# Reordering scatters, pad writes and pair statistics in a one-core conv, attention and expert kernel

## The chip, the cores and the metric

The kernel runs on one core of one Trainium2 chip. The metric is the device time of one execution in microseconds (us). The time before is the median of three runs. Engines are named as in the profile: PE is the matrix engine, DVE the vector engine, ACT the scalar engine, POOL the GpSimd engine and SP the sync engine, which here only issues DMAs.

## The reference

The input x is 32 x 64 x 16 x 16. Three blocks follow each other, all in float32:

```python
x = x + _L0_conv_ref(_gn(x), ...)      # group norm of channel pairs, depthwise 3x3 conv (all weights come out as 1)
t = _to_tokens(x)                      # 8192 tokens of 64 channels
t = t + _L1_attn_ref(_ln_t(t), ...)    # hash buckets, pooled keys and values, 8 heads, GELU feed-forward of 256
t = t + _L1_ffn_ref(_ln_t(t), ...)     # router over 8 experts, top 2, SiLU-gated experts of 682 hidden units
x = _from_tokens(t, x)
```

In the attention block each token picks one of 8 buckets in each of 4 hashes (an argmax over rotated features). The means of the buckets give 32 keys and values per image, and a query attends over them. In the expert block each token goes to its two best experts, each result times its gate.

## The kernel before, in words

The 32 images are taken in 8 groups of 1024 tokens. Every group passes four stages: **a** (group norm, convolution, first layer norm), **b** (buckets, keys, values, scores, attention), **c** (second half of the attention, feed-forward) and **d** (router, places of the rows). The program is a software pipeline written out by hand: in round i group i is in stage a, group i-1 in b, group i-2 in c and group i-3 in d. Each engine has its own list of steps per round and runs it strictly in that order, and semaphores tie the lists together. A step that waits holds up everything behind it on its engine.

Rounds 0 to 4 (`iteration`, run by `ramp`) have no expert work: these are the rounds without tiles. Rounds 5 to 9 (`mixed_iteration`, run by `mix`; MIX is 5) also compute experts. The routed rows (the token twice, the gate and the token's number: 130 floats) are scattered to DRAM by POOL with indirect DMAs (`scatter`, L538), 16 of them for each group. Experts then work on tiles of 256 rows: 71 tiles, cut into two bursts per round. For a tile SP loads weights (`load_weights`, L412) and rows (`load_rows`, L423) three tiles ahead; PE turns the rows (`turn_rows`, L831), ACT copies them (`store_xs`), PE does the up products (`up`, L876), ACT the SiLU (L1135), DVE the product (L1558), PE the down product (L889). POOL scatters the results (L546). The first row load waits until all 16 scatters of group 1 have landed; these are spread over rounds 4 and 5.

Behind each expert's last row the kernel writes a pad of 256 rows, so that its last tile reads harmless rows, and one more pad behind all regions: nine DMAs on SP (`write_pad`, L382). Their places are known once DVE has counted the last group (`pads_ready`, L1522). The first tile that can touch a pad is tile 49, and its row load waits for all nine.

The steps of the pair statistics belong to stage a. `pair_means` and `pair_variances` are two tiny products on PE (L644, L648); `channel_variances` (L1306 to L1308) lies between them on DVE and `pair_statistics` (L1312, L1313) behind them; POOL's `group_rstd` (L482 to L487, a power) follows, then ACT's `normalise_x` (L1027). In stage b, `rotate` (L681) leads to `buckets` (L1355 to L1360), `bucket_sums` (L697), `bucket_means` (L1366 to L1369), `turn_pooled` (L703), `store_pooled` (L1374), `keys` and `values` (L708, L714); `queries` (L688) are copied by ACT (`store_queries`, L1055). In stage c, `sum2`, `total2` and `centre2` (L1405 to L1413) on DVE are followed by `squares2` on ACT (L1087), `variance2` on DVE (L1419, L1420), and the power `rstd2` on POOL (L499). ACT's list has `squares2` and, from round 3 on, `store_wtok` (L1107, which the router's product waits for) ahead of `store_queries`.

Of the kernel before, what the change touches and what calls it, by code (L numbers as in the profile page):

```python
# [19 lines left out]
NE = 8  # L20
# [52 lines left out]
def hybrid_block(nc, x, consts, smalls, weights, out):  # L73
    with ExitStack() as ctx:
# [310 lines left out]
        def _(sp):  # L385
# [14 lines left out]
            def write_pads():  # L400
                sp.wait_ge(pads_ready, 1)
                write_pad(sp, NE * REG)
                for e in range(NE):
                    write_pad(sp, sp.value_load(pad_row[0:1, e:e + 1], min_val=0, max_val=NE * REG - MT))
# [28 lines left out]
            def burst(i, part):  # L433
                for t in range(*BURSTS[i, part]):
                    if t == PADS_AT:
                        write_pads()
                    load_tile(t + W_SLOTS - 1)
# [19 lines left out]
        def _(pool):  # L457
# [118 lines left out]
            def mixed_iteration(i, a=None, b=None, c=None, d=None):  # L576
                if i == MIX:
                    run(c, residual)
                    scatter(MIX - 4, 5, 3)
                    run(d, rstd3)  # L580
                    scatter(MIX - 4, 8, 2)
                    run(c, rstd2)
                    run(a, group_rstd)
                    scatter(MIX - 4, 10, 6)
                    run(b, unit_sum)
                else:
                    run(a, group_rstd)
                    if i == MIX + 1:
                        scatter(MIX - 2, 8, 4)
# [40 lines left out]
        def _(pe):  # L630
# [282 lines left out]
            def iteration(i, a=None, b=None, c=None, d=None, e=None):  # L913
                run(c, attend, 2)
                run(c, attend, 3)
                run(b, turn_n1, 1)
                run(a, pair_means)
                run(b, rotate)
                run(a, pair_variances)
                run(d, turn_wtok)  # L920
                run(b, queries, 0)
                run(b, queries, 1)
# [25 lines left out]
            def mixed_iteration(i, a=None, b=None, c=None, d=None):  # L948
                if i == MIX:
# [16 lines left out]
                    turn_rows(BURSTS[i, 0][0])  # L966
                    turn_rows(BURSTS[i, 0][0] + 1)
                    run(c, fc1, 1)
                    run(c, fc2, 0)
                    run(c, fc2, 1)  # L970
                else:
# [48 lines left out]
        def _(act):  # L1020
# [159 lines left out]
            def mixed_iteration(i, a=None, b=None, c=None, d=None):  # L1180
                if i == MIX:
# [10 lines left out]
                    run(b, key_blocks)  # L1192
                    store_xs(BURSTS[i, 0][0])
                    store_xs(BURSTS[i, 0][0] + 1)
                    run(c, gelus, 1)
# [67 lines left out]
        def _(dve):  # L1263
# [321 lines left out]
            def iteration(i, a=None, b=None, c=None, d=None, e=None):  # L1585
# [7 lines left out]
                run(c, attended, 1)  # L1593
                run(c, sum2)
                run(c, total2)
                run(c, centre2)
                run(d, normalise3)
                run(a, channel_variances)
                run(b, buckets)
                run(a, pair_statistics)  # L1600
                run(c, variance2)
                run(b, bucket_means)
# [124 lines left out]
def run(group, step, *args):  # L1727

    if group is not None:
        step(group, *args)  # L1730
# [37 lines left out]
PADS_AT = BURSTS[NG + 1, 1][0] + 4  # L1768
# [89 lines left out]
```

## Time and profile before

| | |
|---|---|
| median of 3 runs | 767.5 us (766.65 to 769.26) |
| the profiled execution | 771.0 us, its span 769.1 us |
| PE | busy 633.8 us (82%), mean granted clock 0.897 |
| DVE | busy 479.8 us (62%) |
| POOL | busy 369.3 us (48%) |
| ACT | busy 364.0 us (47%) |
| pads | nine DMAs of 130 KB |

The span runs from the first to the last instruction. A granted clock of 1.00 is 2.4 GHz, of 0.50 it is 1.2 GHz. In a row of the timeline the first number is the start, the second the duration, both in us, and the brackets give the idle time before it and what ended that. PE's matmuls are counted as passes there (an fp32 product has two), and neighbouring rows of one kind are merged. The rounds without tiles lie at about 34 to 71 (round 1), 71 to 104 (round 2), 104 to 144 (round 3) and 144 to 187 us (round 4); round 5 up to its first tile lies at 187 to 229 us; the last burst (tiles 40 to 70) begins at 582 us.

### The profile page before, as it was taken

What the parts mean: (1) busy time and instruction counts of PE and PEld (TensorE: products, weight loads), DVE (VectorE), ACT (ScalarE), POOL (GpSimd) and SP (SyncE); (2) the same over time, 40 slices, a digit from 0 to 9 for tenths busy, and PEclk for the clock granted to TensorE, in tenths of its full rate; (3) what the DMA queues carried; (4) which work ended last, traced back from release to release, by engine and by line L of the source; (5) the groups of instructions that cost most, each with busy time, mean ns of one, the idle gap of its engine ahead of it and who ended that gap; (6) DMA issues with size and microseconds to landing.
All of it is one profiled execution on the core that took longest, in us unless ns stands there. A gap on an engine that the chain in (4) does not pass through costs nothing.

```text
span 769.1 us, 14151 instructions
## 1 busy us (share of the span) xinstructions
PE 633.8 (82%) x4582; PEld 474.5 (62%) x4582; DVE 479.8 (62%) x1206; ACT 364.0 (47%) x710; POOL 369.3 (48%) x378
## 2 busy tenths in 40 slices
PE   2497889798559798889999999978978989999950
PEld 1476768667346675658657776756566657777730
DVE  2337677778408775578767877586756535555535
ACT  1133636465426364555557555654554435555520
POOL 2202250776702727764874558444755724444450
PEclk9658887879559899999999999999997989999985
DMA  2000000011132313352341416051542655555509
GB/s 85 5 15 1 15 0 15 18 46 60 35 121 83 124 37 111 117 146 90 107 149 54 160 60 187 18 158 37 183 130 63 188 159 165 161 164 161 165 6 327
DMA packets 46617, 75.50 MB, mean 98 GB/s; under 512 B 7488, under 2 KB 30048, under 8 KB 46544
## 3 DMA queue, kind: packets, MB, share of 16 engines
q1 hardware_dynamic: 35600, 57.67, 25.2%
q0 software_dynamic: 8640, 12.74, 4.8%
q10 hardware_dynamic: 2304, 4.20, 1.4%
q8 instruction: 37, 0.61, 0.3%
q14 instruction: 36, 0.29, 0.1%
HBM read 58.56 MB, written 16.47 MB: 98 GB/s over the span
## 4 chain that ended last, share of the span: by engine, by line
PE 42%; issue 17%; POOL 16%; DVE 15%; ACT 4%; DMA 4%; SPq 2%; POOLq 0%; ACTq 0%; DVEq 0%
PE bk L876 15%; POOL expert_rows L538 9%; PE bk L889 9%; DVE units L1558 3%; PE bk L786 3%; PE bk L660 2%; PE bk L831 2%; PE bk L751 2%; PE bk L725 2%; POOL rr L493 2%; POOL expert_results L546 2%; PE bk L896 1%; PE bk L776 1%; POOL r L499 1%; PE bk L681 1%
## 5 line engine op out<-in xcount | busy, mean ns | idle before, releaser
L876 PE MATMUL bk<-xs,wbuf 64*128 64x256 f32 x1704 | 209.9, 390 | 9.7 <-DVE units L1558 6.1
L546 POOL DMA_INDIRECT expert_results<-yout,xin x142 | 140.8, 992 | 144.8 <-DVE yout L1569 112.7
L1558 DVE TENSOR_TENSOR units<-bk,silu 128x512 f32<-128x512 f32 x213 | 143.9, 689 | 89.1 <-ACT silu L1135 88.5
L876 PEld LDWEIGHTS bk<-xs,wbuf 64*128 64x128 f32 x1704 | 161.6, 189 | 55.0 <-issue 27.0
L1135 ACT ACTIVATE silu<-bk 128x512 f32<-128x512 f32 x213 | 125.1, 596 | 84.9 <-PE bk L876 84.5
L538 POOL DMA_INDIRECT expert_rows<-srow,pos x128 | 130.7, 1021 | 70.7 <-issue 36.0
L889 PE MATMUL bk<-units,wbuf 128*64 128x256 f32 x852 | 108.9, 391 | 3.9 <-DVE ysum L1565 3.5
L889 PEld LDWEIGHTS bk<-units,wbuf 128*64 128x64 f32 x852 | 55.5, 137 | 39.8 <-issue 11.8
L1129 ACT ACTIVATE ysb<-bk 128x256 f32<-128x256 f32 x71 | 27.3, 384 | 86.0 <-PE bk L889 86.0
L493 POOL TENSOR_TENSOR rr<-vare,c_mhalf 128x16 f32<-128x16 f32 x8 | 23.5, 2937 | 83.1 <-DVE vare L1338 83.1
L831 PE MATMUL bk<-const,xin 128*128 128x128 f32 x142 | 30.0, 304 | 22.2 <-DMA xin<-expert_rows 15.1
L831 PEld LDWEIGHTS bk<-const,xin 128*128 128x128 f32 x142 | 15.7, 147 | 44.1 <-issue 26.4
L751 PE MATMUL bk<-vblk,prob_t 128*128 128x144 f32 x256 | 38.1, 302 | 2.9 <-ACT prob_t L1082 2.9
L725 PE MATMUL bk<-kblk,qt 65*128 65x256 f32 x128 | 35.4, 406 | 6.1 <-DVE ssub L1390 6.0
L751 PEld LDWEIGHTS bk<-vblk,prob_t 128*128 128x128 f32 x256 | 34.5, 199 | 6.5 <-ACT prob_t L1082 6.4
L1124 ACT ACTIVATE xs<-bk 128x256 f32<-128x256 f32 x71 | 26.2, 381 | 22.7 <-PE bk L831 22.7
L786 PEld LDWEIGHTS bk<-small,hid 128*128 128x128 f32 x256 | 32.1, 204 | 4.8 <-ACT hid L1098 4.5
L786 PE MATMUL bk<-small,hid 128*128 128x128 f32 (+1 forms) x256 | 32.9, 288 | 2.1 <-ACT hid L1098 2.1
L1075 ACT ACTIVATE prob<-ssub 128x512 f32<-128x512 f32 x32 | 19.7, 627 | 31.0 <-DVE ssub L1390 30.9
L660 PE MATMUL bk<-const,hsum 128*128 128x128 f32 x192 | 34.2, 327 | 0.0
L1563 DVE COPY ysum<-bk 128x128 f32<-128x128 f32 x71 | 20.1, 283 | 22.2 <-PE bk L896 21.6
L504 POOL TENSOR_TENSOR r<-vare,c_mhalf 128x8 f32<-128x8 f32 x8 | 13.8, 1724 | 39.3 <-DVE vare L1439 39.2
(192 smaller groups left out, 979.8 us busy)
## 6 DMA issues: line engine op xcount, KB each, us to landing
wbuf<-in_weights SPq DMA_DIRECT2D x71, 576.0 KB, 4.0
xin<-expert_rows SPq DMA_DIRECT2D x71, 130.0 KB, 3.4
expert_results<-yout,xin POOLq DMA_INDIRECT x142, 3.1
xg<-in_x SPq DMA_DIRECT2D x8, 256.0 KB, 2.8
expert_rows<-srow,pos POOLq DMA_INDIRECT x128, 2.4
srow<-expert_results SPq DMA_DIRECT2D x8, 256.0 KB, 5.3
srow<-expert_results ACTq DMA_DIRECT2D x8, 256.0 KB, 6.3
out<-hid ACTq DMA_DIRECT2D x8, 256.0 KB, 5.6
```

Source lines behind the costliest of these rows:

```text
L493: g.tensor_tensor(rr[:, :, :].rearrange("p a j -> p (a j)"), vare1[:, :, :].rearrange("p a j -> p (a j)"), c_mhalf[:, :], ALU.pow).then_in ...
L538: g.indirect_dma_start(rows[0:NE * REG, :], bass.IndirectOffsetOnAxis(ap=pos[:, d, k, j:j + 1], axis=0), srow[:, d % ROW_SLOTS, k, j, :], ...
L546: g.indirect_dma_start(results[:, :], bass.IndirectOffsetOnAxis(ap=xin[:, t % X_SLOTS, h, ROW - 1:ROW].bitcast(U32), axis=0), yout[:, t % ...
L660: last = mm(o, hsum[:, s, h0 + dy:h0 + dy + 8, :], ident, start=False, stop=dy == 2)
L725: last = mm(bk12[:, p % 2, bp * 256:(bp + 1) * 256], qt[:, j * P:(j + 1) * P], kblk[:, m, :, :].rearrange("c h m -> c (h m)"), start=True, ...
L751: last = mm(bk5[:, at:at + 2 * (C + HEADS)].rearrange("p (r c) -> p r c", r=2), prob_t[:, p % 2, 2 * bp + ch, :], vblk[:, m, ch, :].unsque ...
L786: last = mm(y_of(c)[:, j:j + n, :], hid[:, a, par, q * P:(q + 1) * P], fc2_s[:, a, :].unsqueeze(1).broadcast_to([P, n, C]), start=a == 0, ...
L831: last = turn(xt_of(t)[:, h * P:(h + 1) * P], xin[:, t % X_SLOTS, h, 0:2 * C], ident)
L876: last = mm(bank[:, ch * MT:(ch + 1) * MT], wbuf[part, t % W_SLOTS, at:at + P], xs[part, t % 2, :], start=True, stop=True)
L889: last = mm(y_bank(t)[ch * C:(ch + 1) * C, 0:MT], wbuf[:, t % W_SLOTS, at:at + C], units[:, t % 2, q, ch * MT:(ch + 1) * MT], start=q == 0 ...
L1135: f(silu[:, q, :], h1_ps[q], ACT.Silu).then_inc(silu_ready, 1)
L1558: tt(units[:, t % 2, q, :], h3_ps[q], silu[:, q, :], ALU.mult).then_inc(unit_ready, 1)
```

## The change: what it does

There are four parts.

1. **Pads.** The nine pad writes stood together ahead of the loads of tile 47. Now two stand ahead of the loads of each of tiles 44, 45, 46 and 47, and the ninth ahead of those of tile 48.
2. **Scatters of round 5.** The last eight scatters of group 1 stood as two, then the two powers `rstd2` and `group_rstd`, then six. Now all eight stand ahead of the powers.
3. **First rows of round 5.** `turn_rows` of tiles 0 and 1 moves on PE from between the two halves of `fc1` to behind `fc2`; on ACT `store_xs` moves behind the second `gelus`.
4. **Rounds without tiles.** On PE `rotate` now stands ahead of `pair_means` and `queries` ahead of `pair_variances`. On DVE `buckets`, `channel_variances` and `normalise3` now stand ahead of `sum2`, `total2` and `centre2`, and `bucket_means` ahead of `variance2`.

```diff
-            def write_pads():
+            def write_pads(k):
                 sp.wait_ge(pads_ready, 1)
-                write_pad(sp, NE * REG)
-                for e in range(NE):
+                if k == PAD_STEPS:
+                    write_pad(sp, NE * REG)
+                for e in range(2 * k, min(2 * k + 2, NE)):
                     write_pad(sp, sp.value_load(pad_row[0:1, e:e + 1], min_val=0, max_val=NE * REG - MT))
...
-                    if t == PADS_AT:
-                        write_pads()
+                    if PADS_AT <= t <= PADS_AT + PAD_STEPS:
+                        write_pads(t - PADS_AT)
                     load_tile(t + W_SLOTS - 1)
...
                     run(d, rstd3)
-                    scatter(MIX - 4, 8, 2)
+                    scatter(MIX - 4, 8, 8)
                     run(c, rstd2)
                     run(a, group_rstd)
-                    scatter(MIX - 4, 10, 6)
                     run(b, unit_sum)
...
                 run(b, turn_n1, 1)
+                run(b, rotate)
                 run(a, pair_means)
-                run(b, rotate)
+                run(b, queries, 0)
+                run(b, queries, 1)
                 run(a, pair_variances)
                 run(d, turn_wtok)
-                run(b, queries, 0)
-                run(b, queries, 1)
                 run(b, bucket_sums)
...
                     run(c, fc1, 0)
-                    turn_rows(BURSTS[i, 0][0])
-                    turn_rows(BURSTS[i, 0][0] + 1)
                     run(c, fc1, 1)
                     run(c, fc2, 0)
                     run(c, fc2, 1)
+                    turn_rows(BURSTS[i, 0][0])
+                    turn_rows(BURSTS[i, 0][0] + 1)
...
+                    run(c, gelus, 1)
                     store_xs(BURSTS[i, 0][0])
                     store_xs(BURSTS[i, 0][0] + 1)
-                    run(c, gelus, 1)
...
                 run(c, attended, 1)
+                run(b, buckets)
+                run(a, channel_variances)
+                run(d, normalise3)
                 run(c, sum2)
                 run(c, total2)
                 run(c, centre2)
-                run(d, normalise3)
-                run(a, channel_variances)
-                run(b, buckets)
                 run(a, pair_statistics)
+                run(b, bucket_means)
                 run(c, variance2)
-                run(b, bucket_means)
...
-PADS_AT = BURSTS[NG + 1, 1][0] + 4
+PADS_AT = BURSTS[NG + 1, 1][0] + 1
+PAD_STEPS = NE // 2
```

**POOL, round 5.** Before, between `residual` (x2t) and `unit_sum`; L504 is `rstd3`, L499 `rstd2`, L482 to L487 `group_rstd`:

```order
L538 DMA expert_rows<-srow,pos 67584x130 x3
L504 TENSOR_TENSOR r<-vare,c_mhalf 128x8
L538 DMA expert_rows<-srow,pos 67584x130 x2
L499 TENSOR_TENSOR r<-vare,c_mhalf 128x8
L482 TENSOR_TENSOR grstd<-gvar,c_mhalf 128x2
L484 TENSOR_SCALAR rstd<-grstd 128x2
L485 TENSOR_TENSOR gshift<-gneg,grstd 128x2
L487 TENSOR_SCALAR shift_b<-gshift,small 128x2
L538 DMA expert_rows<-srow,pos 67584x130 x6
```

And now (lines below L406 are counted one higher in the new file):

```order
L539 DMA expert_rows<-srow,pos 67584x130 x3
L505 TENSOR_TENSOR r<-vare,c_mhalf 128x8
L539 DMA expert_rows<-srow,pos 67584x130 x8
L500 TENSOR_TENSOR r<-vare,c_mhalf 128x8
L483 TENSOR_TENSOR grstd<-gvar,c_mhalf 128x2
L485 TENSOR_SCALAR rstd<-grstd 128x2
L486 TENSOR_TENSOR gshift<-gneg,grstd 128x2
L488 TENSOR_SCALAR shift_b<-gshift,small 128x2
L516 TENSOR_TENSOR u_tok<-u_tok,u 128x512
```

Six scatters moved from behind the two powers to ahead of them.

**PE, round 5.** The end of the list up to the first tile (L776 is `fc1`, L786 `fc2`), as a piece of the difference:

```order
 L761 MATMUL bk<-const,n 128x128 x4
 L714 MATMUL bk<-v_aug,pooled_rep 128x128 x4
-L776 MATMUL bk<-n2t,fc_s 128x512 x2
-L831 MATMUL bk<-const,xin 128x128 x4
-L776 MATMUL bk<-n2t,fc_s 128x512 x2
+L776 MATMUL bk<-n2t,fc_s 128x512 x4
 L786 MATMUL bk<-small,hid 128x128 x14
 L786 MATMUL bk<-small,hid 128x64 x2
+L831 MATMUL bk<-const,xin 128x128 x4
 L876 MATMUL bk<-xs,wbuf 128x256 x24
```

The four turns of the first two tiles' rows moved from the middle of `fc1` to just ahead of the tiles.

**DVE, round 2.** Before, from `attended` to `pair_statistics`:

```order
L1399 TENSOR_TENSOR att<-bk,rden 128x256
L1405 TENSOR_TENSOR x<-u,att 128x512
L1410 TENSOR_REDUCE ssum<-x 128x8
L1413 SCALAR_TENSOR_TENSOR cent<-ssum,x 128x512
L1306 TENSOR_TENSOR dmean<-mv,bk 128x2
L1307 TENSOR_TENSOR dmean<-dmean 128x2
L1308 TENSOR_TENSOR chvar<-dmean,mv 128x2
L1355 TENSOR_REDUCE bmax<-bk 128x32
L1356 TENSOR_TENSOR beq<-bk,bmax 128x256
L1358 TENSOR_TENSOR beq<-beq,const 128x256
L1359 TENSOR_REDUCE bfirst<-beq 128x32
L1360 TENSOR_TENSOR onehot<-beq,bfirst 128x256
```

And now (one higher again):

```order
L1356 TENSOR_REDUCE bmax<-bk 128x32
L1357 TENSOR_TENSOR beq<-bk,bmax 128x256
L1359 TENSOR_TENSOR beq<-beq,const 128x256
L1360 TENSOR_REDUCE bfirst<-beq 128x32
L1361 TENSOR_TENSOR onehot<-beq,bfirst 128x256
L1307 TENSOR_TENSOR dmean<-mv,bk 128x2
L1308 TENSOR_TENSOR dmean<-dmean 128x2
L1309 TENSOR_TENSOR chvar<-dmean,mv 128x2
L1406 TENSOR_TENSOR x<-u,att 128x512
L1411 TENSOR_REDUCE ssum<-x 128x8
L1414 SCALAR_TENSOR_TENSOR cent<-ssum,x 128x512
L1313 TENSOR_SCALAR gvar<-bk 128x2
```

The five bucket steps and the three of the channel variances moved ahead of the three that end in the centred tokens (`cent`), and these now stand ahead of `gvar`.

## Rows read from the trace of the kernel before

**Rows 1.** Timeline of SP, 590 to 620 us:

```profile
593.43 0.37 SPq L423 DMA_DIRECT2D xin<-expert_rows  x1
597.14 0.35 SPq L412 DMA_DIRECT2D wbuf<-in_weights  x1
...
603.82 9.99 SPq L382 DMA_DIRECT2D expert_rows<-const  x9
614.65 0.37 SPq L412 DMA_DIRECT2D wbuf<-in_weights  x1
615.80 0.40 SPq L423 DMA_DIRECT2D xin<-expert_rows  x1
```

**Rows 2.** Timeline of PE, 605 to 630 us (L876 starts a tile, L831 turns rows):

```profile
605.89 2.86 PE L876 MATMUL bk<-xs,wbuf 64*128 64x256 f32 x24
...
610.71 2.86 PE L876 MATMUL bk<-xs,wbuf 64*128 64x256 f32 x24
619.07 0.69 PE L831 MATMUL bk<-const,xin 128*128 128x128 f32 x2 [5.50 <-DMA xin<-expert_rows]
...
628.26 2.86 PE L876 MATMUL bk<-xs,wbuf 64*128 64x256 f32 x24
```

**Rows 3.** The row loads (L423), 590 to 640 us:

```profile
DMA to landing us min/median/max: 3.2/3.6/4.2
```

**Rows 4.** Timeline of POOL, round 5:

```profile
195.77 1.44 POOL L538 DMA_INDIRECT expert_rows<-srow,pos  x1 [0.19 <-issue]
...
199.35 1.67 POOL L499 TENSOR_TENSOR r<-vare,c_mhalf 128x8 f32<-128x8 f32 x1 [0.88 <-DVE vare L1420]
...
208.26 0.96 POOL L538 DMA_INDIRECT expert_rows<-srow,pos  x1 [0.31 <-issue]
209.52 0.96 POOL L538 DMA_INDIRECT expert_rows<-srow,pos  x1 [0.30 <-issue]
```

**Rows 5.** Timeline of PE, round 5 up to the first tile:

```profile
203.68 1.08 PE L761 MATMUL bk<-const,n 128*128 128x128 f32 x4 [0.24 <-DVE lsub L1452]
...
206.40 2.08 PE L776 MATMUL bk<-n2t,fc_s 64*128 64x512 f32 x4
...
218.56 0.69 PE L831 MATMUL bk<-const,xin 128*128 128x128 f32 x2 [3.09 <-DMA xin<-expert_rows]
219.18 2.08 PE L776 MATMUL bk<-n2t,fc_s 64*128 64x512 f32 x4
222.61 6.39 PE L786 MATMUL bk<-small,hid 128*128 128x128 f32 x32 [1.35 <-ACT hid L1098]
```

**Rows 6.** Timeline of ACT, the same stretch:

```profile
209.67 2.14 ACT L1069 ACTIVATE kblk<-bk,const 65x128 f32<-65x128 f32 x8
...
222.58 1.28 ACT L1135 ACT_TABLE_LOAD   x1
230.10 0.60 ACT L1135 ACTIVATE silu<-bk 128x512 f32<-128x512 f32 x1 [6.24 <-PE bk L876]
```

**Rows 7.** Windows: us, busy us (instructions) of PE, PEld, DVE, ACT, POOL; PE clock; DMA share; GB/s:

```profile
85.00:105.00 20.00, 19.22 (x139) 16.32 (x137) 14.92 (x31) 12.66 (x20) 3.80 (x2) 1.00 0.00 1
```

**Rows 8.** Timeline of ACT, round 2:

```profile
76.13 0.59 ACT L1055 ACTIVATE qt<-bk 65x512 f32<-65x512 f32 x1 [1.18 <-PE bk L688]
```

**Rows 9.** Timeline of DVE, rounds 2 and 4:

```profile
73.59 0.69 DVE L1413 SCALAR_TENSOR_TENSOR cent<-ssum,x 128x512 f32<-128x512 f32 x1
...
149.05 1.76 DVE L1445 TENSOR_TENSOR wtok<-cent,r 128x512 f32<-128x512 f32 x1 [1.57 <-POOL r L504]
...
159.81 0.23 DVE L1451 TENSOR_REDUCE lmax<-bk 128x8 f32<-128x64 f32 x1 [1.21 <-PE bk L804]
```

**Rows 10.** Timeline of POOL, round 4:

```profile
150.34 1.59 POOL L515 TENSOR_TENSOR u_tok<-u_tok,u 128x512 f32<-128x512 f32 x1
```

**Rows 11.** Timeline of PE, round 4 (the wait for the channel variances):

```profile
145.78 2.03 PE L681 MATMUL bk<-rot_aug,n1t 65*128 65x128 f32 x16
152.20 0.58 PE L648 MATMUL bk<-chvar,const 128*128 128x2 f32 x2 [4.39 <-DVE chvar L1308]
```

## The prediction

> **What bounds the kernel now.** I read the windows first, for the clock and for who is busy where; then the list of waits for each stage; then the timelines around the four places that the change touches. The reader is to see that each stage has its own limit.
>
> In the last burst PE is the limit: a tile takes 610.71 - 605.89 = 4.82 us from one start to the next [rows 2]. One place falls out of this beat: PE stands 5.50 us until the rows of tile 47 land [rows 2]. The reason is on SP. The nine pads occupy it from 603.82 to 613.81, 1.11 us each, and the loads of tile 47 stand behind them: weights at 614.65, rows at 615.80, landed 3.3 us later [rows 1, 2].
>
> In round 5, up to the first tile, the limit is POOL. The last scatter of group 1 starts at 209.52 [rows 4]; only then may SP load the first rows; those of tile 1 are turned at 218.56; the second `fc1` half stands behind that turn, then `gelus`, `fc2` (222.61 to 229.00), and the first tile [rows 5]. PE idles or runs at 1.2 GHz: its 32 passes of `fc2` take 6.39 us.
>
> In the rounds without tiles nothing is saturated. A chain runs through PE, DVE, POOL and ACT, and PE waits in it for the channel variances, 4.39 us in round 4 [rows 11].
>
> **The change part by part.** Times are those of the profiled execution (771.0 us, span 769.1); the median is 3.5 us less, and I carry differences over unchanged. From 230 us on the program only follows its own dependencies, so whatever is gained ahead of that shifts everything behind it.
>
> *Pads.* Tile 46 starts at 610.71 and tile 48 at 628.26. Without the stall tile 48 would start two beats behind tile 46: 610.71 + 2 x 4.82 = 620.35. The loss is 628.26 - 620.35 = 7.9 us: 5.5 of standing, the rest PE work at the lower clock behind it [rows 2]. Now two pads (2 x 1.11 = 2.2 us) go into SP's gap of each tile. The gap is there: the rows of tile 44 are issued at 593.43 (to 593.80) and the weights of tile 45 at 597.14, 3.3 us later [rows 1]. Of these about 0.84 us is the lead-in of a load, as between 613.81 and 614.65, so two pads fill 593.8 to 596.0 and the lead-in ends at 596.9: just inside. The rows have slack too: tile 45's, issued at about 598.3, take 3.2 to 4.2 us to land [rows 3] and are needed 2 us ahead of the tile start at 605.89, at 603.9, so 1.4 to 2.4 us are left. I take the whole 7.9 as gained; the bounds are -7.9 and -3 (each of four tiles slipping 1.2).
>
> The Trainium skill says in "DMA: Bandwidth & Descriptors", section "Queues, rings and completion order", that SP's DMAs share one row of rings and that descriptors on an engine are consumed in ring order, so a load behind pads also waits for their bytes, not only for SP. By the row, the rows issued behind all nine pads landed in 3.3 us, like any other [rows 1, 2], so the trace so far does not bear out a cost; by the rule two pads in front would lengthen four loads, which is the rival "late rows" below.
>
> *Scatters of round 5.* On POOL the eight scatters now run on from 195.77. The first takes 1.44, the others come every 1.26 us (209.52 - 208.26) [rows 4]: the last starts at about 205.1, 4.4 us earlier. The price: `rstd2`, done at 201.0 before, now starts at 206.1 and is done at 207.8, 6.7 us later. DVE's `normalise2` waits for it, with `centre_logits`, `value_blocks` and `centre3` queued behind. So n2 is there at 208.5, the router's bank is read out at 208.9, and `turn_n2`, at 203.68 before, starts at 209.0: +5.3 [rows 5]. `group_rstd` is also later but nobody needs it before the first burst.
>
> *First rows of round 5.* From there, with the durations of before: `values` to 212.0; `fc1` at 212.0; `key_blocks` on ACT 3.27 us behind that (209.67 - 206.40), 215.3 to 217.4; second `fc1` half at about 214.8, which no longer waits for rows; second `gelus` 217.4 to 218.7; `fc2` 218.7 to 225.1 at the low clock [rows 5, 6]. The rows landed long ago (4.4 us earlier, about 214.2), so the two turns (0.69 each) end at 226.5, and the first tile starts there, not at 229.0: -2.5. ACT's table load (1.28 us), hidden under `fc2` before, now stands behind `store_xs`: 227.0 to 228.3. The first SiLU, at 230.10 before, starts then: -1.8 [rows 6]. DVE's `centre3` follows `fc2` and is done at 227.3, earlier than that. I take -2.3 for both parts together; bounds -5 (`fc2` at 2.4 GHz) and +1 (the first tile starts at 1.2 GHz).
>
> *Rounds without tiles.* What the reader may expect is that PE's queries fill the wait for the variances, which they do. But two things come later. `pair_variances` and `pair_statistics` stand behind more work, so POOL's `group_rstd` and ACT's `normalise_x` are late. And `centre2` stands behind the buckets; ACT's `squares2` waits for it, and `store_queries` (and `store_wtok`) queue behind `squares2`.
> Round 1 has no stage c: only `normalise_x` moves, by about the duration of `queries`, 1.4 us, of which the half reaches `values`: +0.7.
> Round 2: `centre2` ended at 73.59 + 0.69 = 74.3, just as `rotate` did [rows 9]. Now, behind `rotate`, DVE does the buckets (five steps, 2.25 us), the variances (0.5) and then `sum2`, `total2` and `centre2` (2.1): it ends at 79.4. The squares end at 80.1, and the first copy of the queries starts then and not at 76.13 [rows 8]. `normalise_x`, `repeat_pooled` and `key_blocks` stand behind it, and of these 4 us about 1.6 was idle time on ACT: +2.4.
> Round 4: `rotate` (145.78 to 147.8 [rows 11], now 0.3 earlier) ends at 147.5, then the buckets at 149.8, the variances at 150.3, `normalise3` at 152.0 (at the 1.7 us that this step took at 149.05 [rows 9]), `centre2` at 154.1, the squares at 154.8, `store_wtok` at 155.3, the router's product (2.1) at 157.4. Its readout, at 159.81 before [rows 9], comes at 157.5: -2.3. Round 3 by the same steps: -1.0.
> Sum of the four: +0.7 + 2.4 - 1.0 - 2.3 = -0.2. As each is a difference of chains some 30 us long, I give it bounds of -6 and +4.
>
> How long `normalise3` takes there is open. It took 1.76 us at 149.05, while POOL was in its own adds up to 150.34 + 1.59 [rows 9, 10]; it is as large as `centre2`, 0.69 [rows 9]. By 1.7 us round 4 gives -2.3, by 0.69 it gives -3.3. The Trainium skill, "SBUF — State Buffer", section "Who interferes with whom", says that a VectorE instruction with two SBUF inputs and a GpSimd instruction that reads SBUF exclude each other for the whole instruction. The trace agrees, and by that rule it is -2.3 here too, since the step now starts right behind POOL's add at 150.34.
>
> *Sum.* -7.9 - 2.3 - 0.2 = -10.4: 760.6 for the profiled execution, 757.1 us for the median.
>
> **The rivals.**
> *Clock kept (faster).* PE's long wait in rounds 3 and 4 is broken up by queries, so the clock may not fall there. In round 4 it was at 1.2 GHz from the wait of 4.39 us on [rows 11]; `fc2`'s 32 passes show what the level costs, 6.39 us there. Some 3 us for each of the two rounds: 757.1 - 6 = 751. Against it: PE still waits, now for `squares2` and `store_wtok`, 2 us in each.
> *Late rows.* The pads lengthen the landing of four loads past their 1.4 to 2.4 us of slack, the stall comes back in pieces of 1.2 us: -3 for -7.9, 762. For it: SP's gap is full to 0.2 us; against it: the 3.3 us behind nine pads.
> *ACT's queue dominates.* The +2.4 of round 2 also holds in rounds 3 and 4, where I have -3.3 in sum: 8 us more, hence 765.
> *Slower: the clock stays down in round 2.* PE now waits at 76.5, at 78.1 and at 80.6 us for variances and queries. In 85 to 105 us PE was busy 19.22 of 20 us at a granted clock of 1.00 [rows 7]. If the clock does not come back until the round is over, this work takes about 1.75 times as long: +14, and 757.1 + 14 = 771. It decides if the level is still 0.50 behind round 2's convolution; below 10 us of such work it is no longer slower. Against it: before, the level came back behind the unbroken `values` and convolution, which are still there.
> *The change does not do what it says*: SP has no gap for two pads and one pair delays the next loads. That is "late rows" again.
>
> **How the numbers follow.** Forecast (757, own range 753.5 to 761): 0.55. Clock kept (751): 0.16. Late rows (762): 0.12. ACT's queue (765): 0.10. Slower (771): 0.07. No change is within 0.3%, 2.3 us, which is about what a measurement of this kernel can tell: 765.2 to 769.8. Half of the queue case falls there or just above its edge, and a little of the slow case: same 0.06, slower 0.06, faster 0.88. The range of 8 in 10 leaves out the slow case and the outer parts of both sides: 750 to 764.
>
> **What would show it.** In the last burst no wait of PE for rows around tile 47 and an unbroken beat of 4.8 us; SP's pads in pairs. In round 5 the last scatter 4 us before, `rstd2` 6 to 7 us later, against the round's start; PE's `fc2` no longer behind a turn, and the SiLU 2 us earlier. In round 2 ACT's `qt` some 4 us later, in round 4 the router's readout 2 us earlier. The prediction is wrong if PE still waits for rows by more than 2 us in the last burst, if the clock of rounds 2 to 4 differs by more than 5 us of low level, or if `normalise2` in round 5 is not what `turn_n2` waits for.

## The result and the profile after

| | before | after |
|---|---|---|
| median (range), 4 runs each | 768.33 us (766.65 to 769.26) | 757.06 us (753.68 to 757.51) |
| profiled execution, its span | 771.0, 769.1 us | 757.51, 755.4 us |
| PE busy, mean granted clock | 633.8 us, 0.897 | 626.2 us, 0.908 |

The ratio is 0.9845, with a 95% interval of 0.9821 to 0.9869: 11.9 us less, 10.1 to 13.8. Forecast were 757.1 us and 10.4 us less.

The table splits the two profiled executions at PE's marks: the start of the second `turn_n1` of each round, the first tile, the first tile of the last burst, and tile 48.

| stretch, us | before | after | difference |
|---|---|---|---|
| round 1 | 36.42 | 35.56 | -0.9 |
| round 2 | 32.55 | 35.46 | +2.9 |
| round 3 | 40.57 | 38.50 | -2.1 |
| round 4 | 42.82 | 41.85 | -1.0 |
| round 5 up to the first tile | 41.91 | 37.31 | -4.6 |
| first tile to last burst | 353.09 | 351.89 | -1.2 |
| last burst up to tile 48 | 46.24 | 39.47 | -6.8 |
| from tile 48 on | 140.84 | 140.82 | 0.0 |

No part of the change touches the stretch from the first tile to the last burst. In the other kernels below it is 351.95 to 354.73 us long, so its -1.2 is not put down to the change.

**The last burst.** SP's timeline of the kernel after; compare [rows 1]:

```profile
585.06 0.37 SPq L413 DMA_DIRECT2D wbuf<-in_weights  x1
586.31 0.39 SPq L424 DMA_DIRECT2D xin<-expert_rows  x1
587.77 1.56 SPq L382 DMA_DIRECT2D expert_rows<-const  x2
590.17 0.37 SPq L413 DMA_DIRECT2D wbuf<-in_weights  x1
```

The pads stand in pairs. PE's timeline, against [rows 2]:

```profile
593.77 2.86 PE L876 MATMUL bk<-xs,wbuf 64*128 64x256 f32 x24
...
596.98 0.44 PE L831 MATMUL bk<-const,xin 128*128 128x128 f32 x2 [0.35 <-DMA xin<-expert_rows]
599.01 2.86 PE L876 MATMUL bk<-xs,wbuf 64*128 64x256 f32 x24
602.90 0.44 PE L831 MATMUL bk<-const,xin 128*128 128x128 f32 x2 [1.03 <-DMA xin<-expert_rows]
604.93 2.86 PE L876 MATMUL bk<-xs,wbuf 64*128 64x256 f32 x24
```

The wait of 5.50 us is gone. Two short ones are new, 0.35 and 1.03 us, and two tiles are 5.24 and 5.92 us behind the one ahead instead of 4.82. They are waits for rows. The row loads between 570 and 640 us, against [rows 3]:

```profile
DMA to landing us min/median/max: 3.4/3.6/5.6
```

The rows of tile 45 are the 5.6: they leave at 591.38 and are turned at 596.98. Those of tile 46 are not in this list; by the chain of the trace they took 6.35 us, from 596.51 to 602.86. The loads are slower in a stretch in which the DMA engines are nearly full. Its window after (us, busy us of PE, PEld, DVE, ACT, POOL, PE clock, DMA share, GB/s):

```profile
593.00:605.00 12.00, 10.62 (x90) 7.22 (x86) 6.75 (x16) 5.12 (x10) 8.71 (x9) 1.00 0.92 255
```

and before, while the last of the nine pads went out, and then while the rows of tile 47 were on their way:

```profile
609.00:615.00 6.00, 4.57 (x40) 3.10 (x37) 3.79 (x8) 2.83 (x6) 3.80 (x4) 1.00 0.48 144
...
617.00:619.00 2.00, 0.00 (x0) 0.00 (x0) 0.00 (x0) 0.00 (x0) 0.00 (x0) 0.56 1.05 327
```

Before, the pads took the place of the loads; now they share the DMA engines with them and with POOL's scatters, at 0.92 of their time. A high share is not the whole cause, though. Before, the rows of tile 47 landed in 3.2 us while the share reached 1.05, but POOL sent nothing from 614 to 622 us. Which of the transfers holds a load up was not tried.

**Round 5.** POOL's timeline, against [rows 4]:

```profile
203.97 0.96 POOL L539 DMA_INDIRECT expert_rows<-srow,pos  x1 [0.30 <-issue]
204.95 1.67 POOL L500 TENSOR_TENSOR r<-vare,c_mhalf 128x8 f32<-128x8 f32 x1
```

The round starts at 185.91 here and at 187.02 before. Counted from there the last scatter is 4.4 us earlier and `rstd2` 6.7 us later. PE's timeline, against [rows 5]:

```profile
207.89 1.09 PE L761 MATMUL bk<-const,n 128*128 128x128 f32 x4 [5.58 <-DVE lsub L1452]
...
213.46 2.65 PE L776 MATMUL bk<-n2t,fc_s 64*128 64x512 f32 x4 [0.77 <-ACT hid L1098]
217.22 5.30 PE L786 MATMUL bk<-small,hid 128*128 128x128 f32 x32 [1.10 <-ACT hid L1098]
222.36 0.61 PE L831 MATMUL bk<-const,xin 128*128 128x128 f32 x4
223.22 5.86 PE L876 MATMUL bk<-xs,wbuf 64*128 64x256 f32 x48 [0.25 <-ACT xs L1124]
```

`turn_n2` waits 5.58 us and starts 5.3 us later than before; `fc2` starts 4.3 us earlier, no longer behind a turn; the first tile starts 4.6 us earlier. ACT's timeline, against [rows 6]:

```profile
223.46 1.28 ACT L1135 ACT_TABLE_LOAD   x1
224.75 1.09 ACT L1135 ACTIVATE silu<-bk 128x512 f32<-128x512 f32 x2
```

The table load is now in the open, and yet the first SiLU is 4.2 us earlier, counted from the round's start.

**Round 2.** ACT's timeline, against [rows 8], with DVE's step that it waits for:

```profile
78.35 0.63 ACT L1087 ACTIVATE sq<-cent 128x512 f32<-128x512 f32 x1 [6.95 <-DVE cent L1413]
78.89 1.06 ACT L1055 ACTIVATE qt<-bk 65x512 f32<-65x512 f32 x2
80.12 1.09 ACT L1027 ACTIVATE xpad<-xg,gshift,grstd 128x256 f32<-128x256 f32 x2 [0.18 <-POOL shift_b L488]
```

```profile
77.62 0.69 DVE L1413 SCALAR_TENSOR_TENSOR cent<-ssum,x 128x512 f32<-128x512 f32 x1
```

`squares2` waits 6.95 us for `centre2`, and both copies of the queries wait behind it, as expected. (In the traces DVE's lines have the same numbers as before; the second list for DVE above shows them one higher.)

**Round 4.** PE's timeline, against [rows 11]:

```profile
151.37 0.38 PE L648 MATMUL bk<-chvar,const 128*128 128x2 f32 x2 [2.03 <-DVE chvar L1308]
...
155.20 2.08 PE L804 MATMUL bk<-small,wtok_t 128*128 128x128 f32 x8 [1.57 <-ACT wtok_t L1107]
...
158.98 2.08 PE L714 MATMUL bk<-v_aug,pooled_rep 65*128 65x128 f32 x8 [0.25 <-ACT pooled_rep L1060]
```

And DVE's, against [rows 9]:

```profile
148.40 1.06 DVE L1358 TENSOR_TENSOR beq<-beq,const 128x256 f32<-128x256 f32 x1
...
149.94 0.91 DVE L1360 TENSOR_TENSOR onehot<-beq,bfirst 128x256 f32<-128x256 f32 x1
...
151.26 0.69 DVE L1445 TENSOR_TENSOR wtok<-cent,r 128x512 f32<-128x512 f32 x1
...
157.31 0.23 DVE L1451 TENSOR_REDUCE lmax<-bk 128x8 f32<-128x64 f32 x1 [1.73 <-PE bk L804]
```

The router's readout comes 2.5 us earlier than before (157.31 against 159.81; the round itself starts 0.14 us earlier), and so does `values`. Only 1.0 is left at the end of the round. From the start of `values` to `fc1` PE takes 10.77 us (158.98 to 169.75), where it took 9.30 (161.49 to 170.79): 1.5 of the 2.5 are lost there. The windows show how. After:

```profile
160.00:170.00 10.00, 10.00 (x57) 9.61 (x58) 6.88 (x25) 5.10 (x13) 7.56 (x9) 0.71 0.26 81
```

and the same stretch before:

```profile
160.00:170.00 10.00, 8.95 (x54) 8.40 (x55) 8.39 (x31) 6.99 (x19) 7.86 (x8) 0.83 0.24 75
```

And the row of `values` before, in PE's timeline:

```profile
161.49 1.16 PE L714 MATMUL bk<-v_aug,pooled_rep 65*128 65x128 f32 x8 [0.51 <-ACT pooled_rep L1060]
```

PE has no idle time there now, at a granted clock of 0.71 instead of 0.83: `values` takes 2.08 us, 1.16 before, and the convolution's first passes run at 1.2 GHz too.

### The profile page after: what moved, and what is told of

It reads as the page before. It is cut to its first block, busy times and chain, and to the rows that moved or that the text cites. A ratio compares the mean times of both kernels' runs of the same rounds, so it can differ in the third digit from the quotient of the medians.

```text
span 755.4 us, 14149 instructions
## 1 busy us (share of the span) xinstructions
PE 626.2 (83%) x4582; PEld 471.4 (62%) x4582; DVE 476.8 (63%) x1206; ACT 362.7 (48%) x710; POOL 366.4 (49%) x378
## 4 chain that ended last, share of the span: by engine, by line
PE 49%; DVE 14%; POOL 14%; issue 13%; ACT 4%; DMA 4%; SPq 1%; POOLq 0%; ACTq 0%; DVEq 0%
PE bk L876 17%; PE bk L889 9%; POOL expert_rows L539 8%; PE bk L786 3%; DVE units L1558 3%; PE bk L660 3%; PE bk L751 2%; PE bk L725 2%; PE bk L831 2%; PE bk L681 2%; PE bk L776 2%; DMA srow<-expert_results 2%; POOL expert_results L547 2%; PE bk L896 1%; PE bk L714 1%
## 5 line engine op out<-in xcount | busy, mean ns | idle before, releaser
L876 PE MATMUL bk<-xs,wbuf 64*128 64x256 f32 x1704 | 209.7, 390 | 8.3 <-DVE units L1558 4.3
L876 PEld LDWEIGHTS bk<-xs,wbuf 64*128 64x128 f32 x1704 | 161.4, 189 | 53.7 <-issue 26.3
L831 PE MATMUL bk<-const,xin 128*128 128x128 f32 x142 | 28.9, 297 | 8.6 <-ACT silu L1135 7.0
L786 PEld LDWEIGHTS bk<-small,hid 128*128 128x128 f32 x256 | 31.0, 199 | 4.6 <-ACT hid L1098 4.3
L786 PE MATMUL bk<-small,hid 128*128 128x128 f32 (+1 forms) x256 | 31.8, 282 | 1.9 <-ACT hid L1098 1.9
L831 PEld LDWEIGHTS bk<-const,xin 128*128 128x128 f32 x142 | 15.5, 145 | 28.6 <-issue 26.0
L1388 DVE TENSOR_REDUCE smax<-bk 128x16 f32<-128x512 f32 x32 | 21.8, 682 | 16.3 <-PE bk L725 16.0
L660 PEld LDWEIGHTS bk<-const,hsum 128*128 128x128 f32 x192 | 31.5, 243 | 0.0
```

The source lines that it names most:

```text
L660: last = mm(o, hsum[:, s, h0 + dy:h0 + dy + 8, :], ident, start=False, stop=dy == 2)
L786: last = mm(y_of(c)[:, j:j + n, :], hid[:, a, par, q * P:(q + 1) * P], fc2_s[:, a, :].unsqueeze(1).broadcast_to([P, n, C]), start=a == 0, ...
L831: last = turn(xt_of(t)[:, h * P:(h + 1) * P], xin[:, t % X_SLOTS, h, 0:2 * C], ident)
L876: last = mm(bank[:, ch * MT:(ch + 1) * MT], wbuf[part, t % W_SLOTS, at:at + P], xs[part, t % 2, :], start=True, stop=True)
```

## The experiments

Ratios are to the kernel before, timed on the same chip, with 95% intervals. The kernel after, timed a second time from the unchanged file (`c0_after`), gave 756.54 us, ratio 0.9826 (0.9796 to 0.9855). Rounds 1 to 4 took 150.8 us and round 5 up to the first tile 37.3, as expected:

> The changed kernel again, beside the others on the same chip, as what the three are compared with: 757, with rounds 1 to 4 in sum at 150.7 us and 37.3 us from round 5's start to the first tile.

Each ratio is known to about 0.003, so two ratios less than about 0.004 (3 us) apart are not told apart by the times, and the lengths of stretches, read as in the table above, have to decide. Round 1 alone, whose steps hardly change, was 33.8 to 36.7 us long from kernel to kernel.

**Pads alone** (`e1_pads`): before, with part 1 (`write_pads` as in the diff of the change).

```diff
...
-                    if t == PADS_AT:
-                        write_pads()
+                    if PADS_AT <= t <= PADS_AT + PAD_STEPS:
+                        write_pads(t - PADS_AT)
...
-PADS_AT = BURSTS[NG + 1, 1][0] + 4
+PADS_AT = BURSTS[NG + 1, 1][0] + 1
+PAD_STEPS = NE // 2
```

> The kernel before with the first part of the change alone, the pads two at a time. From the two traces, tile 48 came 6.8 us nearer to the start of the last burst, and PE still waited twice for rows (0.35 and 1.03 us). Theory: the part is worth what these rows say wherever it stands, -6.8 us against before (-6 to -7.5), about 761.5. Rival 1, the full 7.9 of the prediction: the two waits would be gone, below 760.5. Rival 2, the late rows of the prediction: -3, about 765.

Measured: 762.07 us, ratio 0.9904 (0.9874 to 0.9935), so 7.4 us less, 5.0 to 9.7; the table has 6.8. Its own last burst up to tile 48 is 39.01 us long, 7.2 less than before, with one wait for rows, 0.62 us.

This stretch varies. In the eight kernels with the pads in pairs it is 38.08 to 39.47 us long, and with the nine together 46.24 (before) and 45.76 (`e11_rows_only`), so against before the part is worth 6.8 to 8.2 us. PE waits for rows there twice (after, 0.35 and 1.03; the same file in `c0_after`, 0.89 and 0.43), once or, in `e4_undo_ramp`, not at all.

**Without the early scatters** (`e2_undo_scatter`): after, with part 2 undone.

```diff
-                    scatter(MIX - 4, 8, 8)
+                    scatter(MIX - 4, 8, 2)
                     run(c, rstd2)
                     run(a, group_rstd)
+                    scatter(MIX - 4, 10, 6)
```

> The changed kernel with its second part undone: two scatters, the two powers, six scatters. Theory: moving the scatters costs, since normalise2 and turn_n2 wait 5 us for the power, and once turn_rows stands behind fc2 the rows have time to land. With the durations of the changed kernel's trace turn_n2 would start at 202.6 and not 207.9, fc2 end at 218.4 and the first tile start at 219.8 and not 223.2: -3.4 us against the changed kernel (-1.5 to -4.5), about 753.7. Rival: the scatters are what feeds the first tile; rows of tile 1 come at 217.5 to 218.5 plus two turns, and the slow DMA lets nothing be gained or costs up to 2: 757 to 759.

Measured: 751.84 us, ratio 0.9767 (0.974 to 0.9794), faster than after. Its PE timeline (lines one higher), where round 5 starts at 184.08:

```profile
200.73 1.09 PE L762 MATMUL bk<-const,n 128*128 128x128 f32 x4 [0.24 <-DVE lsub L1453]
...
210.07 6.12 PE L787 MATMUL bk<-small,hid 128*128 128x128 f32 x32 [1.11 <-ACT hid L1099]
216.02 0.61 PE L832 MATMUL bk<-const,xin 128*128 128x128 f32 x4
216.88 5.87 PE L877 MATMUL bk<-xs,wbuf 64*128 64x256 f32 x48 [0.26 <-ACT xs L1125]
```

and its load of the first rows on SP:

```profile
212.01 0.38 SPq L424 DMA_DIRECT2D xin<-expert_rows  x1
```

The rows of tile 1 leave at 212.01 and are turned behind `fc2` at 216.02 without a wait. Round 5 is 32.80 us long, 4.5 shorter than after. The expectation was 3.4. So with the turns behind `fc2` the late scatters cost nothing any more, and the early ones only delay `turn_n2`.

**Without the moved turns** (`e3_undo_rows`): after, with part 3 undone.

```diff
                     run(c, fc1, 0)
+                    turn_rows(BURSTS[i, 0][0])
+                    turn_rows(BURSTS[i, 0][0] + 1)
                     run(c, fc1, 1)
                     run(c, fc2, 0)
                     run(c, fc2, 1)
-                    turn_rows(BURSTS[i, 0][0])
-                    turn_rows(BURSTS[i, 0][0] + 1)
...
-                    run(c, gelus, 1)
                     store_xs(BURSTS[i, 0][0])
                     store_xs(BURSTS[i, 0][0] + 1)
+                    run(c, gelus, 1)
```

> The changed kernel with its third part undone: turn_rows of tiles 0 and 1 and their copies stand between the halves of fc1 again. Theory: with the scatters early the rows have landed by then (about 213), so the turns only push the second half of fc1 and ACT's second gelus by 0.7 us, while the table load is hidden under fc2 again: -0.5 to +0.7 us, no difference that can be told, about 757. Rival: the move is needed even with early scatters, since rows land later than the trace suggests: +2.5, about 759.5.

Measured: 758.44 us, ratio 0.9842 (0.9815 to 0.9869), not to be told from after; round 5 is 38.46 us, 1.2 longer. Part 2 by itself is thus worth some 3 us there (41.91 or 41.0 in two kernels without either part, 38.46 with it). This is read across kernels that differ in part 4 or part 1 too; part 2 alone was not run.

**The moved turns alone** (`e11_rows_only`): before, with part 3 (the edit of the last one in reverse).

> The kernel before with the third part of the change alone: turn_rows of tiles 0 and 1 behind fc2 on PE, their copies behind the second gelus on ACT. Theory: this part carries the gain of round 5 and the early scatters give back part of it, so alone it cuts the stretch from round 5's start to the first tile from 41.5 to 33 us: -8.5 against before (-7 to -9.5), a ratio of 0.989. Rival, as I predicted: the two parts need each other, since the rows come 4 us later without the early scatters: -2.3 or less, a ratio of 0.997.

Measured: 760.48 us, ratio 0.9873 (0.9844 to 0.9903), so 9.8 us less, 7.5 to 12.0. Round 5 is 32.20 us against 41.91. PE's wait of 5.66 us for the rows of tile 47 is still there, as it must be without part 1. So parts 2 and 3 each gain alone, -3 and -9.7; together they gain 4.6, because part 3 takes away the wait that part 2 was for.

**Old order of the rounds without tiles** (`e4_undo_ramp`): after, with part 4 undone.

```diff
+                run(a, pair_means)
                 run(b, rotate)
-                run(a, pair_means)
+                run(a, pair_variances)
+                run(d, turn_wtok)
                 run(b, queries, 0)
                 run(b, queries, 1)
-                run(a, pair_variances)
-                run(d, turn_wtok)
...
-                run(b, buckets)
-                run(a, channel_variances)
-                run(d, normalise3)
                 run(c, sum2)
                 run(c, total2)
                 run(c, centre2)
+                run(d, normalise3)
+                run(a, channel_variances)
+                run(b, buckets)
                 run(a, pair_statistics)
+                run(c, variance2)
                 run(b, bucket_means)
-                run(c, variance2)
```

> The changed kernel with its fourth part undone, the order of the rounds without tiles as before. Theory: the part is worth almost nothing in sum (rounds 1 to 4 end 1.1 us earlier in the changed kernel's trace, of which one is a clock that fell at another moment in round 1): undone it costs 0 to +1.2 us, about 757.6. Rival 1, ACT's queue (squares2 ahead of the copies of the queries) dominates: -2, about 755. Rival 2, the queries in PE's wait keep the clock up: +4 or more.

Measured: 756.4 us, ratio 0.9828 (0.9801 to 0.9855): the same as after. By rounds, as means of three kernels with each order (old: before, pads alone, this one; new: after, and the two before it that undo parts 2 and 3):

| us | round 1 | round 2 | round 3 | round 4 | sum |
|---|---|---|---|---|---|
| old order | 35.11 | 32.86 | 40.19 | 42.82 | 150.98 |
| new order | 35.14 | 35.31 | 38.40 | 41.80 | 150.65 |
| difference | 0.0 | +2.4 | -1.8 | -1.0 | -0.3 |

Three more kernels have one of the two orders. `c0_after` and `e6_pads7` (new) agree with their row. `e11_rows_only` (old) does not: its rounds are 36.57, 35.04, 39.45 and 42.83 us long. In its round 2 PE did the queries at 1.2 GHz, here against the row before:

```profile
76.32 3.65 PE L688 MATMUL bk<-n1t,q_aug 65*65 65x512 f32 x4
```

```profile
75.04 1.91 PE L688 MATMUL bk<-n1t,q_aug 65*65 65x512 f32 x4
```

With all nine kernels the differences are -0.2, +1.9, -1.6 and -1.0, in sum -0.9. So the signs of rounds 2 to 4 hold, and the +2.4 of round 2 is known only to about 1 us.

**Queries ahead of the squares on ACT** (`e5_squares`): after, with `squares2` behind `store_queries`.

```diff
                 run(b, store_queries, 1)
+                run(c, squares2)
...
                     run(a, store_n1t, 1)
-                    run(b, squares2)
                     run(c, store_wtok)
```

> The changed kernel with one ACT step moved in the rounds without tiles: squares2 stands behind the two copies of the queries instead of at the end of the round before. Theory (ACT's queue): in round 2 the copies start when the queries are there (about 75) and not at 78.9, in rounds 3 and 4 the copy of the router's tokens and with it the router come 1.5 to 2 us earlier. But normalise_x also waits for POOL and pair_statistics behind centre2, so not all of it shows. Rounds 2, 3 and 4 shorter by 0.5 to 1.5, 1 to 2 and 1 to 2 us: -3.5 against the changed kernel (-1.5 to -5.5), about 753.5. Rival: it is DVE's order (pair_statistics and bucket_means behind centre2) that sets rounds 2 to 4, and ACT's queue is hidden: no change, 757, with round 2 still at 35.3 us.

Measured: 754.76 us, ratio 0.9808 (0.9776 to 0.9839), not to be told from after. Rounds 3 and 4 are 0.6 and 2.0 us shorter, round 5 is 1.2 longer (why is open), and round 2 stays at 35.25, where 34 to 35 was expected. Its ACT in round 2:

```profile
73.59 0.59 ACT L1055 ACTIVATE qt<-bk 65x512 f32<-65x512 f32 x1 [3.17 <-PE bk L688]
...
77.36 0.63 ACT L1087 ACTIVATE sq<-cent 128x512 f32<-128x512 f32 x1 [2.32 <-DVE cent L1413]
79.14 1.09 ACT L1027 ACTIVATE xpad<-xg,gshift,grstd 128x256 f32<-128x256 f32 x2 [1.15 <-POOL shift_b L488]
```

The queries are copied early, and `normalise_x` still waits, now for POOL. So ACT's queue was one of two chains of nearly equal length in round 2, and its removal alone gives nothing there.

**`centre2` ahead of the buckets** (`e9_centre`): after, with `sum2`, `total2` and `centre2` back ahead of `buckets`, the rest of part 4 kept.

```diff
                 run(c, attended, 1)
-                run(b, buckets)
-                run(a, channel_variances)
-                run(d, normalise3)
                 run(c, sum2)
                 run(c, total2)
                 run(c, centre2)
+                run(b, buckets)
+                run(a, channel_variances)
+                run(d, normalise3)
```

> The changed kernel with one group of DVE steps moved in the rounds without tiles: sum2, total2 and centre2 ahead of buckets, as in the kernel before; all else of the fourth part stays. Theory: the price of the fourth part is centre2 behind the buckets, which holds up pair_statistics on DVE (and with it POOL's power and normalise_x) as much as squares2 on ACT; DVE has room for the three steps (2.1 us) while PE does rotate. Then round 2 goes from 35.3 to 33 us, round 3 from 38.4 to 36.5 to 37.5, round 4 from 41.8 to 39 to 40: -5.5 against the changed kernel (-4 to -7.5), about 751. Rival: round 2 is long because pair_variances stands behind the queries on PE, whatever DVE does: round 2 stays at 35.3 and the kernel gains what late squares gave, -2, 755.

Measured: 752.86 us, ratio 0.9784 (0.9758 to 0.9809): 3 us less than after by the ratios, at the edge of what they tell, where 5.5 was expected. Rounds 2, 3 and 4 are 34.57, 36.66 and 41.23 us long, 0.9, 1.8 and 0.6 less than after. In round 2, PE's, DVE's and ACT's timeline:

```profile
77.66 0.38 PE L648 MATMUL bk<-chvar,const 128*128 128x2 f32 x2 [0.92 <-DVE chvar L1308]
```

```profile
78.08 0.16 DVE L1312 TENSOR_SCALAR gvar<-bk 128x2 f32<-128x2 f32 x1 [0.48 <-PE bk L648]
```

```profile
79.98 1.09 ACT L1027 ACTIVATE xpad<-xg,gshift,grstd 128x256 f32<-128x256 f32 x2 [2.61 <-POOL shift_b L488]
```

Now ACT waits 2.61 us for POOL. `channel_variances` stands behind the five bucket steps on DVE, and PE, done with the queries, waits 0.92 us for it. So it is DVE's order and not the queries ahead of `pair_variances` (the rival) that holds this chain. Round 2 is still 1.7 us longer than in the table's old order (1.1 in `e10_best` below), and this chain is what the traces leave for it; `channel_variances` ahead of `buckets` was not tried.

**Pads seven and two** (`e6_pads7`): after, with seven pads ahead of tile 44's loads, before the burst is in its beat, and two ahead of tile 45's.

```diff
-                if k == PAD_STEPS:
+                if k == 1:
                     write_pad(sp, NE * REG)
-                for e in range(2 * k, min(2 * k + 2, NE)):
+                for e in range(7 * k, min(7 * k + 7, NE)):
...
-                    if PADS_AT <= t <= PADS_AT + PAD_STEPS:
+                    if PADS_AT <= t <= PADS_AT + 1:
```

> The changed kernel with seven pads ahead of the loads of tile 44 and two ahead of those of tile 45. In the changed kernel's trace SP is idle from 578 to 585 there, room for seven. Theory: loads 46 to 48 have no pad in front, PE's two waits for rows (0.35 and 1.03 us) go: -1.3 us against the changed kernel, about 755.7. Rival: seven pads make the loads of tiles 44 and 45 land late, and the waits only move: no change, about 757.

Measured: 756.08 us, ratio 0.9815 (0.9785 to 0.9846), not to be told from after. In the last burst PE waits once, 0.36 us, and the stretch up to tile 48 is 38.34 us long. That shows no gain: four kernels with the pads in pairs also have one wait only, `e4_undo_ramp` has none and 38.08 us, and `e8_sum` below, with seven and two, waits 1.30 us and has 39.48. SP's timeline:

```profile
576.90 7.77 SPq L382 DMA_DIRECT2D expert_rows<-const  x7
...
587.24 1.69 SPq L382 DMA_DIRECT2D expert_rows<-const  x2
```

Here PE is still in the two first tiles of the burst, with rows loaded ahead, and SP has time for seven pads.

**Sums.** Two kernels put the findings together: `e8_sum` (late scatters, late squares, pads seven and two) and `e10_best` (late scatters, `centre2` ahead of the buckets, pads seven and two). Their edits are those shown.

> The changed kernel with three edits together: the scatters of round 5 as they were before (two, powers, six), squares2 behind the copies of the queries, and the pads as seven and two. If the parts add up: -5.2 (measured for the scatters), -3.5 and -1.3 by my theories: about 747. If only the scatters count: 752.

> The same, with the scatters of round 5 as before (two, powers, six) and the pads as seven and two: the candidate for the best version. If all adds up: -5.5 (centre2), -5.2 (scatters), -0.6 (pads): 745.5 (743.5 to 748). If the gain of rounds 2 to 4 is lost on POOL in round 5, which is busy from its start to the last scatter: 751.

Measured: 748.42 us (746.83 to 749.37), ratio 0.9712 (0.9684 to 0.974), and 748.16 us (745.67 to 755.36), ratio 0.9737 (0.9699 to 0.9775). Both beat the kernel before and the kernel after. The two are not told apart from each other, and `e10_best` not from `e2_undo_scatter` (0.9767), which has only the late scatters; it also missed its expectation of 745.5 by 2.7 us. What its other edits add is thus read from the lengths of the rounds and not from the times.

## Why the prediction was right, point by point

The time was off by less than 0.1 us, and part of that is luck: by the ratio the change is worth 11.9 us and by the two profiled executions 13.7, where 10.4 was forecast, and two terms missed in opposite directions. The median before also moved, from 767.5 to 768.33 us, with a fourth run.

*Pads: right, a little small.* -7.9 was forecast, the trace after has -6.8, the others with pairs -6.8 to -8.2. After, the two waits made two tiles 1.5 us longer in sum, and the first two tiles of the burst were 0.4 us shorter. The waits are the rival "late rows" in its mild form: two loads used up the whole 1.4 to 2.4 us of slack, since they took 5.6 and 6.35 us to land, where 4.2 was the most before. The unbroken beat of 4.8 us that the prediction wanted to see is not there, but each wait is under its 2 us. That landing takes longer beside the other transfers is read from the traces; which of them held a load up was not tried. The 3.3 us behind nine pads misled me: these had gone out one every 1.11 us with no load among them, at a share of 0.48, and POOL's scatters stood still while the rows landed. The Trainium skill says in "DMA: Bandwidth & Descriptors", section "Queues, rings and completion order", that descriptors are consumed in ring order; the 5.6 and 6.35 us after do not speak against it, and the 3.2 us before show no cost of it.

*Round 5: the step that was mis-sized, -2.3 forecast and -4.6 measured.* The mechanism held to a tenth up to `turn_n2`: last scatter 4.4 us earlier, `rstd2` 6.7 later, `turn_n2` 5.3 later. `fc2` started 31.3 us into the round for 31.7 forecast; 0.3 of that is my addition, which put `values` and `turn_n2` at 3.0 us where the rows have 2.72 (203.68 to 206.40). What failed is the end: I had `fc2` at the full 1.2 GHz time of 6.4 us and two turns of 0.69, 7.8 in sum up to the first tile; it was 6.0, which is 1.8 of the 2.3 missed. The granted clock rose inside `fc2` (5.30 us), and the four passes took 0.61. The bound of -5 stood for this and was nearer. The greater miss is one that the sum hides: I priced parts 2 and 3 as one. By themselves they are worth -9.7 (part 3) and about -3 (part 2), and on top of part 3, part 2 costs 4.5. My own numbers had it: +5.3 for `turn_n2`, and rows that before were turned at 218.56, while without part 2 `fc2` would end at about 219.8 (my 225.1 less 5.3).

*Rounds without tiles: the sum right (-0.3 for -0.2), the parts only in sign.* Round 1 was forecast at +0.7 and did not change. Round 2 is +2.4 as forecast (+1.9 with all nine kernels), but ACT's queue is not the reason by itself: without it (`e5_squares`) the chain over DVE's buckets and `channel_variances`, PE's `pair_variances` and POOL's power is as long. `centre2` back ahead of the buckets gave 0.9, and 1.7 stayed. Round 3 gained 1.8 for 1.0. Round 4's readout came 2.5 us earlier for 2.3, and 1.0 reached the end of the round, since `values` and the convolution then ran at 1.2 GHz for longer. I had followed the chain to the readout and taken the rest as carried over unchanged.

*Normalise3 and POOL.* `normalise3` took 0.69 us, not 1.7: POOL's second add ran from 149.24 to 150.58 us, and the step came behind it, at 151.26. But two bucket steps fell into these adds and took 1.06 and 0.91 us instead of 0.42. These 1.1 us in sum are what `normalise3` had lost before (1.76 for 0.69), so -2.3 was right for the wrong row.

*Rivals.* "Clock kept" did not come: in round 4 the clock was 0.61 in 150 to 160 us and 0.71 in the next ten, where it was 0.51 and 0.83 before. "ACT's queue dominates" is refuted by rounds 3 and 4, which got shorter, though `squares2` ahead of the queries' copies costs 2.6 us in them (0.6 and 2.0 in `e5_squares`). "Slower" did not come: in round 2 the clock was back before the convolution was over, with 0.6 us lost in it (one six-pass piece took 1.44 us for 0.87).

## What to carry over

When two edits of a change act on one wait, price each with and without the other: the second may turn the first from a gain into a cost. Where work is moved past a wait on one engine, follow the chain to the end of the stage and not to the first readout that comes early, and look for a second chain of nearly the same length before a queue gets the blame. The landing time of a DMA is a price only for the traffic in which it was read: 3.2 us behind pads alone became 5.6 and 6.35 among pads, weights and scatters. And a wait of half a microsecond that goes away in one trace is no gain until the stretch is shorter than it is in the other kernels that have the same code there.

## What was not expected of the hardware

**VectorE steps beside GpSimd work.** In `e10_best` the step L1359 (L1358 in the kernel before) took 2.01 us for 0.42. DVE's and POOL's timeline:

```profile
144.04 2.01 DVE L1359 TENSOR_TENSOR beq<-beq,const 128x256 f32<-128x256 f32 x1
146.09 0.42 DVE L1360 TENSOR_REDUCE bfirst<-beq 128x32 f32<-128x256 f32 x1
```

```profile
142.38 2.12 POOL L505 TENSOR_TENSOR r<-vare,c_mhalf 128x8 f32<-128x8 f32 x1
144.49 1.27 POOL L510 TENSOR_TENSOR u_tok<-tok,small 128x512 f32<-128x512 f32 x1
145.84 1.33 POOL L516 TENSOR_TENSOR u_tok<-u_tok,u 128x512 f32<-128x512 f32 x1
```

It starts while POOL is in its power, ends 0.3 us behind the first add, and the one-input reduction that follows takes its usual 0.42 beside the second. The Trainium skill, "SBUF — State Buffer", section "Who interferes with whom", has a VectorE instruction with two SBUF inputs and a GpSimd instruction that reads SBUF exclude each other; these rows agree, and so the cost of such a DVE step depends on where POOL's work falls.

**The clock differs from kernel to kernel in the same work.** At the end of round 1, which no part changes there, before:

```profile
66.32 1.12 PE L673 MATMUL bk<-const,n 128*65 128x128 f32 x4 [0.79 <-DVE n L1344]
67.23 4.02 PE L751 MATMUL bk<-vblk,prob_t 128*128 128x144 f32 x16
```

and the kernel with the pads alone:

```profile
66.27 0.65 PE L674 MATMUL bk<-const,n 128*65 128x128 f32 x4 [1.24 <-DVE n L1345]
66.76 2.13 PE L752 MATMUL bk<-vblk,prob_t 128*128 128x144 f32 x16
```

The same 20 passes take 4.9 or 2.6 us. PE's longest wait ahead of them, for `prob` at 64.4 us, is 2.26 us in the one and 2.25 us in the other. What decides between the two is open; round 1, which hardly changes, is 33.8 to 36.7 us long, a spread of 3 us and more than part 4 is worth.
